# Divisions four chunks ahead, and weights and residuals loaded during the attentions, in two output projections

## The chip, the cores and the metric

One core of a Trainium2 chip runs the whole kernel in one launch. The metric is the time on the device in microseconds (us), lower is better. Five engines work side by side, each through its own queue in order: TensorE (PE: matmuls and transposes), VectorE (DVE), ScalarE (ACT), GpSimd (POOL) and SyncE (SP, which here only issues DMAs). They meet through semaphores.

## The reference

x is [2, 256, 48, 48], that is 2 images of 2304 positions and 256 channels. Two layers follow each other; all is float32.

```python
# layer 0: top-k attention, 8 heads of 32, and an MLP of 1x1 convolutions with batch norm
q, k, v = heads(Wq x + bq), heads(Wk x + bk), heads(Wv x + bv)
scores = q k^T * 32 ** -0.5
kth = top_k(scores, 64)[..., -1:]
attn = softmax(where(scores >= kth, scores, min))
o = Wo (attn v) + bo + x
h1 = relu(batchnorm(W1 o + b1));  h2 = batchnorm(W2 h1 + b2)       # 1024 hidden channels
x1 = h2 + o
# layer 1: RMS norm over channels, full attention, output projection
q, k, v = split(w_qkv (x1 / |x1| * g * 16))
out = w_out (softmax(q * 32 ** -0.5 k^T) v) + b_out + x1
```

## The kernel before

`build()` runs seven stages, each a block of its own with one program per engine; an engine leaves a block when all of it is done, so stages do not overlap except by what they load.

1. `project_heads` (layer 0) writes queries and keys, split in a high and a rest part, to DRAM (`q_parts`, `k_parts`) and keeps the values in `v_top`, which lies in the same memory as the big buffer `xs`.
2. `attention_top`: 8 heads times 18 pairs of 128-query tiles. SP loads keys and queries per head (`load_key_parts`, `load_query_parts`); GpSimd copies a head's values out of `v_all` into `v_s` and counts `v_ready`, twice per head. The unnormalised outputs are kept in `o_top`, and the sums of the exponentials in `sums`.
3. `project_out` (L707): 4608 positions in nine chunks of 512. It divides by the sums, turns the outputs so that channels lie on partitions, multiplies by Wo and adds bias and x.
4. `mlp`: first matrix (L874), statistics, relu (L924), second matrix (L889), statistics, x1 and the norm of layer 1. x1 is written to DRAM. One buffer `m_w` holds in turn the first matrix, the second (L859) and the three of the next layer (L818).
5. `project_heads` (layer 1) out of that buffer.
6. `attention_full`: as 2, with a full softmax; its values lie in `v_all`.
7. `output` (L1283): as 3, with w_out, b_out and, as residual, x1 read back from DRAM into `y` (2 transfers of 2304 KB); each finished piece of a chunk is stored to `out`.

The bodies of 3 and 7 are alike. VectorE computes one reciprocal of all 288 sums per partition (L779, L1366), divides chunks 0 and 1 (L777, L1364) and then, for each chunk, does the two adds (L791, L1377; they read the projection from PSUM and write over the residual) and divides chunk c + 2. TensorE turns chunk c + 1 (`turn`: eight transposes, L743, L1331) and projects chunk c (four matmuls of 128x128 by 512, which the trace shows as eight records, L758, L1345). ScalarE copies the turned chunk from PSUM into one of two buffers `a` (L770, L1357); it waits for projection c - 2 before it writes over a buffer. There are four PSUM banks for turned blocks and four for projections. SP issues all loads of such a stage when it begins: in 3 w_o, b_o, x in three pieces (into `xs`, where the values lay before) and the first MLP weights with seven vectors; in 7 w_out, b_out and y. VectorE waits for w and, in 7, for all of y (L1371) before its first add.

Of the kernel before, what the change touches and what calls it, by code (L numbers as in the profile page):

```python
# [26 lines left out]
P = 128  # L27
B, C, N = 2, 256, 48 * 48
KC = C // P
# [243 lines left out]
def attention_top(nc, cst, operands, q_parts, k_parts, v_all, o_all, sums):  # L273
# [5 lines left out]
    with ctx:  # L279
# [45 lines left out]
        def _(sync):  # L325
# [14 lines left out]
            per_head(HEADS - 1, HEADS - 1)  # L340
            for n in range(AHEAD_Q):
                sync.wait_ge(q_loaded[n], 32 * (HEADS * HEAD_PAIRS // AHEAD_Q + 1))
# [364 lines left out]
def project_out(nc, cst, xs, o_all, sums, x, w_o, b_o, mlp_weights, next_sources):  # L707
# [4 lines left out]
    with ctx:  # L712
        sb = lambda name, shape, dt=F32: ctx.enter_context(nc.sbuf_tensor("r_" + name, shape, dt))
        sem = lambda name: ctx.enter_context(nc.semaphore("r_" + name))
        w, bias = sb("w", [P, KC, C]), sb("bias", [P, KC])
# [4 lines left out]
        w_loaded, x_loaded = sem("w_loaded"), [sem(f"x_loaded{n}") for n in range(len(X_PIECES))]  # L720
# [52 lines left out]
        def _(dve):  # L773
# [5 lines left out]
            dve.reciprocal(one_by_sum[:, :, :], sums[:, :, :]).then_inc(inverse_ready, 1)  # L779
            dve.wait_ge(inverse_ready, 1)  # L780
            divide(0)
            divide(1)
            dve.wait_ge(w_loaded, 32)
            for c in range(NCH):
# [8 lines left out]
                if c + 2 < NCH:  # L793
                    divide(c + 2)
# [27 lines left out]
def mlp(nc, cst, xs, x1, weights, w_2, next_sources):  # L822
# [5 lines left out]
    with ctx:  # L828
# [5 lines left out]
        w2_s = w[:, :].rearrange("p (k c) -> p k c", k=MT)  # L834
# [185 lines left out]
def attention_full(nc, cst, operands, q_parts, k_parts, v_all, o_all, sums):  # L1020
# [7 lines left out]
    with ctx:  # L1028
# [22 lines left out]
        def _(sync):  # L1051
# [14 lines left out]
            per_head(HEADS - 1, HEADS - 1)  # L1066
            for n in range(AHEAD_Q):
                sync.wait_ge(q_loaded[n], 32 * (HEADS * HEAD_PAIRS // AHEAD_Q + 1))
# [214 lines left out]
def output(nc, cst, o_all, sums, x1, w_out, b_out, out):  # L1283
# [4 lines left out]
    with ctx:  # L1288
        sb = lambda name, shape, dt=F32: ctx.enter_context(nc.sbuf_tensor("o_" + name, shape, dt))
        sem = lambda name: ctx.enter_context(nc.semaphore("o_" + name))  # L1290
        w, bias = sb("w", [P, KC, C]), sb("bias", [P, KC])
        one_by_sum = sb("one_by_sum", [P, B * MCH, HEADS])
        a, y = [sb(f"a{n}", [P, KC, CW]) for n in range(2)], sb("y", [P, KC, B * N])
        ps_t = [ctx.enter_context(nc.psum_tensor(f"o_ps_t{n}", [P, CW], F32)) for n in range(4)]
        ps = [ctx.enter_context(nc.psum_tensor(f"o_ps{n}", [P, CW], F32)) for n in range(4)]
        w_loaded, x_loaded = sem("w_loaded"), sem("x_loaded")
# [152 lines left out]
```

## Time and profile before

| | us |
|---|---|
| median of 3 runs | 5311.72 (5310.89 to 5313.05) |
| profiled execution | 5306.61 |
| its span, first to last instruction | 5304.80 |

| engine | busy us | share of the span |
|---|---|---|
| TensorE | 4161.1 | 78% |
| VectorE | 4384.5 | 83% |
| ScalarE | 4144.0 | 78% |
| GpSimd | 1502.1 | 28% |

Where the stages lie in the span: the first attention ends at about 3378, project_out at 3441, mlp at 3772, the second attention at about 5231, output at 5304.8. The granted TensorE clock is a mean of 0.825 of its full 2.4 GHz over the span; a stretch at 0.5 is one at 1.2 GHz. Starts are us from the span's start. A row's "idle before" is the time for which its engine had nothing to do just before it, and behind the arrow stands what ended that.

### The profile page before, as it was taken

Reading aid. Unit: us, or ns where it says so; the run is one execution under the profiler, and the core shown is the slowest. Engines: PE = TensorE matmul, PEld = TensorE weight load, DVE = VectorE, ACT = ScalarE, POOL = GpSimd, SP = SyncE. Lnnn points to the kernel's source line nnn. Section 1 sums busy time; section 2 is a strip of 40 time slices with the busy share of each in tenths; the row PEclk is TensorE's granted clock in tenths of the full one; section 3 lists DMA queues with packets and bytes.
Section 4 is the critical chain, followed back from the end, with each engine's and each line's share of the span. In section 5 each row is a group of like instructions: output and inputs, shape, how many; then the busy total and the mean of one; then the engine's idle time right before and its main releaser. Section 6 shows DMA issues by size and latency. Waiting matters only on the chain. (4 is left out here: it accounts for less than half of the span.)

```text
span 5304.8 us, 112543 instructions
## 1 busy us (share of the span) xinstructions
PE 4161.1 (78%) x32161; PEld 2808.6 (53%) x32161; DVE 4384.5 (83%) x25258; ACT 4144.0 (78%) x6082; POOL 1502.1 (28%) x362
## 2 busy tenths in 40 slices
PE   8576477776777557767777667798999999999997
PEld 4344345444444334444454445443567777777774
DVE  4899999998999899999999999430378888888885
ACT  2798599988998678988999889544268888888884
POOL 0354354444454334444454445100100000000000
PEclk9677677777777777777777777899799999999999
DMA  5000000000000000000000000100320101111012
GB/s 208 6 17 16 5 16 8 18 16 7 18 17 16 7 15 8 17 16 8 17 17 9 17 16 8 56 8 6 143 77 25 34 24 33 33 25 34 24 33 89
DMA packets 79566, 154.52 MB, mean 29 GB/s; under 512 B 8120, under 2 KB 49464, under 8 KB 73528
## 3 DMA queue, kind: packets, MB, share of 16 engines
q1 hardware_dynamic: 78904, 146.72, 9.8%
q8 instruction: 290, 4.75, 0.4%
q14 instruction: 372, 3.05, 0.2%
HBM read 99.50 MB, written 47.19 MB: 28 GB/s over the span
## 5 line engine op out<-in xcount | busy, mean ns | idle before, releaser
L539 POOL TENSOR_TENSOR a_probs<-a_scores,a_probs 128x2304 f32<-128x2304 f32 x288 | 1460.1, 5092 | 1778.5 <-ACT a_probs L462 1778.5
L557 DVE MAX8 a_top<-a_scores 128x8 f32<-128x36 f32 x18432 | 1830.8, 179 | 46.8 <-ACT a_scores L446 46.1
L373 PE MATMUL a_ps_t<-ident,a_probs 128*128 128x128 f32 x5184 | 973.7, 325 | 704.0 <-ACT a_probs_t L457 570.1
L373 PEld LDWEIGHTS a_ps_t<-ident,a_probs 128*128 128x128 f32 x5184 | 672.6, 164 | 992.2 <-ACT a_probs_t L457 708.6
L462 ACT ACTIVATE a_probs<-a_scores,a_steep_kth 128x2304 f32<-128x2304 f32 x290 | 641.2, 2211 | 295.0 <-DVE a_minus_max L667 295.0
L1117 PE MATMUL b_ps_t<-ident,b_soft 128*128 128x128 f32 x5184 | 744.1, 279 | 20.9 <-issue 19.3
L1242 DVE TENSOR_SCALAR_CACHE_REDUCE b_soft<-b_ps_s 128x2304 f32<-128x2304 f32 x288 | 735.2, 2553 | 26.9 <-PE b_ps_s L1101 9.0
L457 ACT ACTIVATE a_probs_t<-a_ps_t 128x512 f32<-128x512 f32 (+1 forms) x1440 | 727.2, 545 | 20.4 <-PE a_ps_t L373 7.4
L1117 PEld LDWEIGHTS b_ps_t<-ident,b_soft 128*128 128x128 f32 x5184 | 581.0, 141 | 204.0 <-issue 80.4
L1199 ACT ACTIVATE b_soft<-b_soft,b_minus_max 128x2304 f32<-128x2304 f32 x288 | 638.1, 2216 | 43.6 <-issue 26.0
L450 ACT ACTIVATE a_probs<-a_probs,a_minus_max 128x2304 f32<-128x2304 f32 x288 | 638.0, 2215 | 28.6 <-issue 18.5
L363 PE MATMUL a_ps_s<-a_k_stack,a_q_ring 128*128 128x512 f32 (+1 forms) x1465 | 647.5, 601 | 14.7 <-ACT a_scores L446 9.8
L446 ACT ACTIVATE a_scores<-a_ps_s 128x2304 f32<-128x2304 f32 x292 | 607.0, 2079 | 12.3 <-PE a_ps_s L363 12.3
L382 PE MATMUL a_ps_o<-a_probs_t,a_v 128*32 128x128 f32 x10368 | 579.0, 303 | 0.2
L1206 ACT ACTIVATE b_soft_t<-b_ps_t 128x512 f32<-128x512 f32 (+1 forms) x864 | 419.4, 520 | 174.6 <-PE b_ps_t L1117 174.3
L363 PEld LDWEIGHTS a_ps_s<-a_k_stack,a_q_ring 128*128 128x128 f32 x1465 | 433.2, 319 | 156.6 <-ACT a_scores L446 64.5
L1101 PE MATMUL b_ps_s<-b_k_stack,b_q_ring 128*128 128x512 f32 (+1 forms) x1440 | 451.0, 411 | 8.4 <-DVE b_soft L1242 5.0
L1248 DVE COPY b_soft_t<-b_ps_t 128x512 f32<-128x512 f32 x576 | 385.1, 687 | 83.1 <-PE b_ps_t L1117 82.7
L382 PEld LDWEIGHTS a_ps_o<-a_probs_t,a_v 128*32 128x32 f32 x10368 | 263.0, 115 | 226.0 <-issue 113.7
L1078 POOL COPY b_v<-v_all 128x576 f32 x16 | 10.6, 667 | 1293.1 <-PE b_ps_o L1136 1185.8
L1136 PE MATMUL b_ps_o<-b_soft_t,b_v 128*32 128x256 f32 x5184 | 368.5, 384 | 0.6 <-issue 0.6
L401 PE MATMUL a_ps_o<-add_up,a_parts 128*128 128x32 f32 x576 | 148.6, 397 | 259.1 <-ACT a_parts L522 259.1
(128 smaller groups left out, 4216.7 us busy)
## 6 DMA issues: line engine op xcount, KB each, us to landing
a_k_stack<-k_parts SPq DMA_DIRECT2D x72, 288.0 KB, 6.0
b_k_stack<-k_parts SPq DMA_DIRECT2D x72, 288.0 KB, 6.1
a_q_ring<-q_parts SPq DMA_DIRECT2D x294, 64.0 KB
b_q_ring<-q_parts SPq DMA_DIRECT2D x294, 64.0 KB
k_parts<-p_high SPq DMA_DIRECT2D x36, 256.0 KB, 2.1
k_parts<-p_rest SPq DMA_DIRECT2D x36, 256.0 KB, 2.2
q_parts<-p_high SPq DMA_DIRECT2D x36, 256.0 KB, 2.0
q_parts<-p_rest SPq DMA_DIRECT2D x36, 256.0 KB, 2.0
```

The source lines that it names most:

```text
L363: last = pe.matmul(ps_s[:, c:c + n], q_ring[pair % AHEAD_Q][:, P * (s % 2):P * (s % 2) + P], k_stack[b][:, c:c + n], start=True, stop=True)
L373: last = pe.transpose(ps_t[(NTG * s + g) % 2][:, P * m:P * m + P], probs[s % 2][:, P * (m0 + m):P * (m0 + m) + P], cst["ident"][:, :])
L382: last = pe.matmul(ps_o[rows, P * (s % 2):P * (s % 2) + P], v_s[s // MCH][:, m, :], probs_t[:, m, :], start=m < 4, stop=m + 4 >= MCH)
L446: act.activation(scores_all[:, s % 4, :], ps_s[:, 0:N], ACT.Copy).then_inc(scores_kept, 1)
L450: act.activation(probs[s % 2][:, :], probs[s % 2][:, :], ACT.Exp, scale=SCALE, bias=minus_max[parity][:, s % 2:s % 2 + 1], accum_out=sums[ ...
L457: act.activation(probs_t[:, m0:m0 + n, :], ps_t[(NTG * s + g) % 2][:, 0:n * P].rearrange("p (m q) -> p m q", q=P), ACT.Copy).then_inc(turn ...
L462: act.activation(probs[u][:, :], scores_all[:, 2 * parity + u, :], ACT.Relu, scale=-STEEP, bias=steep_kth[parity][:, u:u + 1]).then_inc(pe ...
L539: pool.tensor_tensor(probs[u][:, :], scores_all[:, 2 * (p % 2) + u, :], probs[u][:, :], ALU.subtract).then_inc(masked_ready, 1)
L557: last = dve.max(top8[s // 2 % 2][:, s % 2, c, :], scores_all[:, s % 4, CHUNK * c:CHUNK * c + CHUNK])
L1117: last = pe.transpose(ps_t[(NTG * s + g) % 2][:, P * m:P * m + P], soft[s % 3][:, P * (m0 + m):P * (m0 + m) + P], cst["ident"][:, :])
L1199: act.activation(soft[s % 3][:, :], soft[s % 3][:, :], ACT.Exp, scale=-1.0, bias=minus_max[s % 3][:, 0:1], accum_out=sums[:, s, cols(h + a ...
L1242: dve.tensor_scalar(soft[s % 3][:, :], ps_s[:, 0:N], -SCALE, None, ALU.mult, ALU.min, accum_out=minus_max[s % 3][:, 0:1]).then_inc(shifted ...
```

## The change

- Both projections: the reciprocal is split in the part of chunk 0 (32 sums per partition) and the rest (256). Division 0 follows the first part, divisions 1 to 3 the second, and in the loop chunk c + 4 is divided behind chunk c.
- A class `ProjectionOut` holds weights, bias and their semaphores outside of the stage. The loads that SP issued when the stage began are issued in a function `load_ahead` by SP at the end of its program in the attention before, after a wait for `v_ready` to be full (all values have been copied out): for project_out also x into `xs` and the first MLP weights, for output also y.
- y now lies in `v_all` of the second attention, which is kept beyond it, and w_out in the buffer of the key weights of layer 1. w and bias of project_out are allocated ahead of the attention's tiles.
- mlp: the second matrix has a buffer of its own (8 KB per partition), and its load is issued at the start of the stage. The loads of the next layer's weights wait for the first matrix to be done instead of the second.

```diff
@@ attention_top and attention_full, SP
             per_head(HEADS - 1, HEADS - 1)
+            sync.wait_ge(v_ready, HEADS * B)
+            load_ahead(sync)
@@
+DIVIDED_AHEAD = 4
+class ProjectionOut:
+    def __init__(self, nc, ctx, layer, w=None):
+        sb = lambda name, shape: ctx.enter_context(nc.sbuf_tensor(layer + name, shape, F32))
+        self.w = sb("w", [P, KC, C]) if w is None else w
+        self.bias = sb("bias", [P, KC])
+        self.w_loaded = ctx.enter_context(nc.semaphore(layer + "w_loaded"))
+        self.x_loaded = [ctx.enter_context(nc.semaphore(f"{layer}x_loaded{n}")) for n in range(len(X_PIECES))]
+    def load(self, sync, w, bias):
+        sync.dma_start(self.w[:, :, :], w.rearrange("(k p) o -> p k o", p=P)).then_inc(self.w_loaded, 16)
+        sync.dma_start(self.bias[:, :], bias).then_inc(self.w_loaded, 16)
@@ project_out
-        @block.sync
-        def _(sync):
-            sync.dma_start(w[:, :, :], w_o.rearrange("(k p) o -> p k o", p=P)).then_inc(w_loaded, 16)
-            sync.dma_start(bias[:, :], b_o).then_inc(w_loaded, 16)
-            for n in range(len(X_PIECES)):
-                load_x(sync, xs, x, n, x_loaded)
-            mlp_weights.load(sync, next_sources)
@@ project_out and output, VectorE
-            dve.reciprocal(one_by_sum[:, :, :], sums[:, :, :]).then_inc(inverse_ready, 1)
+            dve.reciprocal(one_by_sum[:, 0:4, :], sums[:, 0:4, :]).then_inc(inverse_ready, 1)
             dve.wait_ge(inverse_ready, 1)
             divide(0)
-            divide(1)
+            dve.reciprocal(one_by_sum[:, 4:B * MCH, :], sums[:, 4:B * MCH, :]).then_inc(inverse_ready, 1)
+            dve.wait_ge(inverse_ready, 2)
+            for c in range(1, DIVIDED_AHEAD):
+                divide(c)
@@
-                if c + 2 < NCH:
-                    divide(c + 2)
+                if c + DIVIDED_AHEAD < NCH:
+                    divide(c + DIVIDED_AHEAD)
@@ mlp
-        w2_s = w[:, :].rearrange("p (k c) -> p k c", k=MT)
+        w2_s = sb("w2", [P, MT, C])
@@
+            sync.dma_start(w2_s[:, :, :], w_2.rearrange("(k p) o -> p k o", p=P)).then_inc(w2_loaded, 16)
             sync.wait_ge(hid_done, NCH * MT)
-            sync.dma_start(w2_s, w_2.rearrange("(k p) o -> p k o", p=P)).then_inc(w2_loaded, 16)
-            sync.wait_ge(y_done, NCH * KC)
             weights.load_next(sync, next_sources)
@@ output, SP
-            sync.dma_start(w[:, :, :], w_out.rearrange("(k p) o -> p k o", p=P)).then_inc(w_loaded, 16)
-            sync.dma_start(bias[:, :], b_out).then_inc(w_loaded, 16)
-            for kc in range(KC):
-                sync.dma_start(y[:, kc, :], x1[kc * P:kc * P + P, :]).then_inc(x_loaded, 16)
@@ build
+            projection = ProjectionOut(nc, top, "r_")
+            def load_ahead(sync):
+                projection.load(sync, t["w_o"], t["b_o"])
+                for n in range(len(X_PIECES)):
+                    load_x(sync, xs, t["x"], n, projection.x_loaded)
+                mlp_weights.load(sync, t)
@@
+        v_all = ctx.enter_context(nc.sbuf_tensor("v_all", [P, B * MCH, C], F32))
+        y = v_all[:, :, :].rearrange("p m c -> p (m c)").rearrange("p (k n) -> p k n", k=KC)
+        projection = ProjectionOut(nc, ctx, "o_", mlp_weights.next_w[:, 0, :, :])
@@
+            def load_ahead(sync):
+                projection.load(sync, t["w_out"], t["b_out"])
+                for kc in range(KC):
+                    sync.dma_start(y[:, kc, :], x1[kc * P:kc * P + P, :]).then_inc(projection.x_loaded[0], 16)
```

## Rows read from the trace of the kernel before

**Rows 1.** The page's first line: the span and its instructions.

```profile
span 5304.8 us, 112543 instructions
```

**Rows 2.** The chain of waits that ended last: start us, us, what; its one transfer.

```profile
5233.25 15.22 DMA o_y<-x
```

**Rows 3.** Timeline of output(): start us, us, engine, line, out<-in, count [idle before, releaser].

```profile
5231.60 1.95 DVE L1366 RECIPROCAL o_one_by_sum<-xs 128x288 f32<-128x288 f32 x1 [0.33 <-PEq L1028]
...
5234.96 3.24 PE L1331 MATMUL o_ps_t<-ident,o_all 128*128 128x128 f32 x16 [4.15 <-DVE o_all L1364]
...
5238.04 3.60 PE L1345 MATMUL o_ps<-o_a,o_w 128*128 128x512 f32 x8
...
5258.12 1.22 DVE L1364 TENSOR_TENSOR o_all<-o_all,o_one_by_sum 128x1024 f32<-128x1024 f32 x1
...
5259.39 1.09 PE L1331 MATMUL o_ps_t<-ident,o_all 128*128 128x128 f32 x8 [1.98 <-DVE o_all L1364]
...
5260.32 3.60 PE L1345 MATMUL o_ps<-o_a,o_w 128*128 128x512 f32 x8
...
5263.96 0.75 DVE L1377 SCALAR_TENSOR_TENSOR o_y<-o_ps,o_bias,o_y 128x512 f32<-128x512 f32 x1 [0.97 <-PE o_ps L1345]
...
5264.62 1.22 DVE L1364 TENSOR_TENSOR o_all<-o_all,o_one_by_sum 128x1024 f32<-128x1024 f32 x1
...
5301.60 0.75 DVE L1377 SCALAR_TENSOR_TENSOR o_y<-o_ps,o_bias,o_y 128x512 f32<-128x512 f32 x1 [0.96 <-PE o_ps L1345]
```

**Rows 4.** One line's instructions (L1010): durations in ns, minimum/median/maximum, first and last start.

```profile
L1010 DVE RECIPROCAL m_norm<-m_norm x1: 378/378/378, 3747.6 to 3747.6; 128x36 f32<-128x36 f32 x1
```

**Rows 5.** Timeline of project_out(), same columns; its head, second projection and last add.

```profile
3378.15 1.95 DVE L779 RECIPROCAL r_one_by_sum<-sums_top 128x288 f32<-128x288 f32 x1 [29.63 <-PEq L279]
...
3380.13 2.36 DVE L777 TENSOR_TENSOR o_top<-o_top,r_one_by_sum 128x1024 f32<-128x1024 f32 x2
...
3381.41 3.31 PE L743 MATMUL r_ps_t<-ident,o_top 128*128 128x128 f32 x16 [3.59 <-DVE o_top L777]
...
3384.56 3.60 PE L758 MATMUL r_ps<-r_a,r_w 128*128 128x512 f32 x8
...
3391.08 5.28 PE L758 MATMUL r_ps<-r_a,r_w 128*128 128x512 f32 x8
...
3440.54 0.75 DVE L791 SCALAR_TENSOR_TENSOR xs<-r_ps,r_bias,xs 128x512 f32<-128x512 f32 x1 [0.97 <-PE r_ps L758]
```

**Rows 6.** Stretches: length, busy us (instructions) by engine, granted clock, DMA share, GB/s.

```profile
3378.00:3385.00 7.00, 3.59 (x18) 3.35 (x19) 4.31 (x3) 1.92 (x4) 0.00 (x0) 0.56 0.80 257
3385.00:3392.00 7.00, 5.02 (x18) 2.48 (x17) 2.63 (x3) 1.45 (x3) 0.00 (x0) 0.93 1.02 427
3480.00:3520.00 40.00, 40.00 (x95) 17.75 (x94) 16.12 (x24) 16.04 (x24) 0.00 (x0) 1.00 0.00 0
```

**Rows 7.** Timeline of SP's queue: the last key loads of both attentions.

```profile
3322.83 1.90 SPq L145 DMA_DIRECT2D a_k_stack<-k_parts  x4
5216.58 1.83 SPq L145 DMA_DIRECT2D b_k_stack<-k_parts  x4
```

**Rows 8.** Timeline of GpSimd: two pairs of tiles of the first attention's last head.

```profile
3309.88 10.14 POOL L539 TENSOR_TENSOR a_probs<-a_scores,a_probs 128x2304 f32<-128x2304 f32 x2 [10.76 <-ACT a_probs L462]
3330.36 10.14 POOL L539 TENSOR_TENSOR a_probs<-a_scores,a_probs 128x2304 f32<-128x2304 f32 x2 [10.34 <-ACT a_probs L462]
```

**Rows 9.** Second MLP weights: their load by its line and its landing; what started then.

```profile
L859 SPq DMA_DIRECT2D m_w<-w x1: 378/378/378, 3566.0 to 3566.0; - x1
DMA to landing us min/median/max: 5.4/5.4/5.4
3571.09 11.38 ACT L924 ACTIVATE m_hid<-m_hid,m_shift,m_scale 128x512 f32<-128x512 f32 x16 [0.87 <-DVE m_shift L986]
3572.05 13.48 PE L889 MATMUL m_ps_o<-m_hid,m_w 128*128 x27 [6.05 <-ACT m_hid L924]
```

**Rows 10.** One line's instructions (L557), columns as in rows 4.

```profile
L557 DVE MAX8 a_top<-a_scores x18432: 168/179/201, 116.1 to 3338.3; 128x8 f32<-128x36 f32 x199
```

More of the change, by code:

```diff
@@ L704, in _, with project_out @@
             dve.sem_inc(kth_ready, 1)
-def project_out(nc, cst, xs, o_all, sums, x, w_o, b_o, mlp_weights, next_sources):
+DIVIDED_AHEAD = 4
[9 more added lines that the diff above has]
+        sync.dma_start(self.bias[:, :], bias).then_inc(self.w_loaded, 16)
+def project_out(nc, cst, xs, o_all, sums, projection):
     CW = BANK
@@ L714, in project_out @@
         sem = lambda name: ctx.enter_context(nc.semaphore("r_" + name))
-        w, bias = sb("w", [P, KC, C]), sb("bias", [P, KC])
+        w, bias, w_loaded, x_loaded = projection.w, projection.bias, projection.w_loaded, projection.x_loaded
         one_by_sum = sb("one_by_sum", [P, B * MCH, HEADS])
@@ L1066, in _ @@
             per_head(HEADS - 1, HEADS - 1)
+            sync.wait_ge(v_ready, HEADS * B)
+            load_ahead(sync)
             for n in range(AHEAD_Q):
@@ L1280, in _, with output @@
                 add_quadrants(p, HEADS - 1, (HEADS - 1) * HEAD_PAIRS + p)
-def output(nc, cst, o_all, sums, x1, w_out, b_out, out):
+def output(nc, cst, o_all, sums, y, projection, out):
     CW = BANK
@@ L1290, in output @@
         sem = lambda name: ctx.enter_context(nc.semaphore("o_" + name))
-        w, bias = sb("w", [P, KC, C]), sb("bias", [P, KC])
+        w, bias, w_loaded, x_loaded = projection.w, projection.bias, projection.w_loaded, projection.x_loaded[0]
         one_by_sum = sb("one_by_sum", [P, B * MCH, HEADS])
-        a, y = [sb(f"a{n}", [P, KC, CW]) for n in range(2)], sb("y", [P, KC, B * N])
+        a = [sb(f"a{n}", [P, KC, CW]) for n in range(2)]
         ps_t = [ctx.enter_context(nc.psum_tensor(f"o_ps_t{n}", [P, CW], F32)) for n in range(4)]
         ps = [ctx.enter_context(nc.psum_tensor(f"o_ps{n}", [P, CW], F32)) for n in range(4)]
-        w_loaded, x_loaded = sem("w_loaded"), sem("x_loaded")
         turned, a_ready, proj_done, added, stored = (sem("turned"), sem("a_ready"), sem("proj_done"), sem("added"),
@@ L1364, in divide @@
                 dve.tensor_tensor(o_c, o_c, inverse_c, ALU.mult).then_inc(divided, 1)
-            dve.reciprocal(one_by_sum[:, :, :], sums[:, :, :]).then_inc(inverse_ready, 1)
+            dve.reciprocal(one_by_sum[:, 0:4, :], sums[:, 0:4, :]).then_inc(inverse_ready, 1)
             dve.wait_ge(inverse_ready, 1)
             divide(0)
-            divide(1)
+            dve.reciprocal(one_by_sum[:, 4:B * MCH, :], sums[:, 4:B * MCH, :]).then_inc(inverse_ready, 1)
+            dve.wait_ge(inverse_ready, 2)
+            for c in range(1, DIVIDED_AHEAD):
+                divide(c)
             dve.wait_ge(w_loaded, 32)
@@ L1402, in build @@
             sums = top.enter_context(nc.sbuf_tensor("sums_top", [P, B * MCH, HEADS], F32))
-            attention_top(nc, cst, operands, q_parts, k_parts, v_top, o_top, sums)
-            project_out(nc, cst, xs, o_top, sums, t["x"], t["w_o"], t["b_o"], mlp_weights, t)
+            projection = ProjectionOut(nc, top, "r_")
[4 more added lines that the diff above has]
+                mlp_weights.load(sync, t)
+            attention_top(nc, cst, operands, q_parts, k_parts, v_top, o_top, sums, load_ahead)
+            project_out(nc, cst, xs, o_top, sums, projection)
         mlp(nc, cst, xs, x1, mlp_weights, t["w_2"], (t["w_k1"], t["w_q1"], t["w_v1"]))
@@ L1407, in build @@
         sums = xs[:, 0, 0, 0:B * MCH * HEADS].rearrange("p (m h) -> p m h", h=HEADS)
+        v_all = ctx.enter_context(nc.sbuf_tensor("v_all", [P, B * MCH, C], F32))
+        y = v_all[:, :, :].rearrange("p m c -> p (m c)").rearrange("p (k n) -> p k n", k=KC)
+        projection = ProjectionOut(nc, ctx, "o_", mlp_weights.next_w[:, 0, :, :])
         with ExitStack() as full:
             operands = Operands(nc, full, "b_")
-            v_all = full.enter_context(nc.sbuf_tensor("v_all", [P, B * MCH, C], F32))
             project_heads(nc, xs, mlp_weights.next_w, mlp_weights.next_loaded, operands, q_parts, k_parts, v_all)
-            attention_full(nc, cst, operands, q_parts, k_parts, v_all, o_all, sums)
-        output(nc, cst, o_all, sums, x1, t["w_out"], t["b_out"], out)
+            def load_ahead(sync):
+                projection.load(sync, t["w_out"], t["b_out"])
+                for kc in range(KC):
+                    sync.dma_start(y[:, kc, :], x1[kc * P:kc * P + P, :]).then_inc(projection.x_loaded[0], 16)
+            attention_full(nc, cst, operands, q_parts, k_parts, v_all, o_all, sums, load_ahead)
+        output(nc, cst, o_all, sums, y, projection, out)
 def per_partition(v, rows=P):
```

9 lines of the change are left out of this document (4 added, 5 removed).

## The prediction

> **What bounds the kernel now.** I looked first at the span [rows 1]; the profiled execution took 5306.61 us around a span of 5304.80 us, and the median of the runs shown is 5311.72 us, so the sum below is made on the profiled execution and its difference is carried to the median. The page's share of busy time says little here: the two attentions fill some 4,600 us of the span (the first ends at 3378, the second takes the 1,350 us up to 5231), and this change does not edit what they do. It edits the two short stages behind them and one load inside the MLP. So the second view is the chain that ended last. It shows one transfer of 15.22 us, the residual y of the last stage, on which everything waits [rows 2]. The third view is the timeline of the two stages.
>
> In a steady chunk of output() [rows 3] there are four links in a circle: VectorE divides a chunk (starts 5258.12), TensorE turns it (5259.39), TensorE projects it (5260.32), VectorE adds bias and residual (last one 5263.96), and only then divides the next: 5264.62, which is 6.50 us after the first. TensorE itself is needed for the stretch from 5259.39 to 5263.75: 0.93 us for eight transposes, then eight matmul records that start 0.43 us apart (the row's 3.60 us is seven such steps and the last one's modelled 0.59 us), 3.43 us; the last add starts 0.21 us after that. That is 4.36 us. The other 2.14 us of each period TensorE waits for a division that could have been made earlier. project_out() has the same body. This is the idle time to win.
>
> **Part 1: divisions four chunks ahead.** What is late next, if the division is not? Per chunk VectorE has two adds of 0.75 us and one division of 1.22 us, 2.7 us; ScalarE two copies of 0.6 us; both fit under 4.36 us. The two a buffers let ScalarE fill chunk c+1 once projection c-1 is done, which is just when its transposes are done, and it has the 3.43 us of projection c for 1.2 us of copies. So TensorE is next, back to back: nine projections of 3.43 us, and the seven turns of chunks 2 to 8 between them at 0.93 us: 30.87 + 6.51 = 37.38 us from the first projection on.
>
> The head of each stage gets a reciprocal in two parts. A reciprocal of 36 elements took 0.38 us [rows 4], one of 288 took 1.95 us [rows 5]; between them an element costs 0.0062 us, so 32 elements are 0.36 us and 256 are 1.75 us (estimates from those rows). In project_out: VectorE starts at 3378.15, division 0 at 3378.54 instead of 3380.13, ending 3379.75. Then comes the second reciprocal (3379.69 to 3381.44), and division 1 ends at 3382.69, where it ended at 3382.5 before: the first turn is earlier, the second is not. TensorE turned 16 blocks in 3.15 us at the start [rows 5], thus 8 in 1.58 us, and the first projection starts at 3382.75 + 1.58 = 3384.33 (before: 3384.56). The same working in output [rows 3], from 5231.60: second turn at 5236.19, plus 1.54 us, first projection at 5237.73 (before: 5238.04). Divisions 2 and 3 now stand ahead of the first add on VectorE's queue; they end 2.4 us after division 1, at 3385.1 and 5238.6, and the first add is released 1.7 us into the first projection, at the earliest at 3386.0 and 5239.4, so nobody waits for them.
>
> **The clock at the head.** From 3378 to 3385 the granted clock was 0.56 and thereafter mostly near 1.0, and under a steadily busy TensorE (3480 to 3520) it was 1.00 [rows 6]. In project_out the second projection ran low: eight matmuls in 5.28 us, 5.11 us by the same count, where 3.43 is the full-speed figure [rows 5], 1.7 us more. Before, the 16 transposes came in one piece ahead of the first projection; now there is a hole of 1.3 us between the two turns, so the first projection may also run low. Its price is 0 to 1.7 us; no row is nearer to one end, and I take the middle, 0.85 us, once per stage. Later dips I put at none, because the waits that precede them go.
> The Trainium skill (TensorE: Matmul & The Clock Gate, HAM oscillation) says that a kernel which alternates short bursts with waits is throttled again and again. The trace agrees (0.56 in the first window, 1.00 in the dense MLP), and by that rule alone the sum would be the same without the 0.85 us in each head.
>
> project_out: 3384.33 + 0.85 + 37.38 + 0.21 = 3422.77 for the start of the last add, against 3440.54 [rows 5]: 17.8 us. MLP follows that add as before.
> output: 5237.73 + 0.85 + 37.38 + 0.21 = 5276.17 against 5301.60 [rows 3]: 25.4 us. What follows the last add (its 0.75 us, the last store, the end) stays.
>
> **Part 2: weights and residuals loaded while the attentions still run.** In project_out this brings nothing by itself: the first projection waited for the second turn, and no add waited for x (all adds there are released by TensorE). In output it is needed, or the 25.4 us are not to be had: the first add stood until y had landed at 5248.47 [rows 2]. The loads are queued on SP behind the last key loads, which are issued by 3324.73 and 5218.41 [rows 7]. The wait on v_ready ahead of them is for copies made at the start of the last head, so it holds nothing. In the first attention some 5.8 MB follow; y moved 4.7 MB in 15.2 us, so these take about 19 us and end some 30 us before that stage starts. In the second, y is issued at about 5219.4 and lands between 5234.6 and, with the 1.2 MB of keys still ahead of it at the same rate, 5238.5. The first add wants it at 5239.4; TensorE would first be stopped at the projection of chunk 2, which needs the first of four PSUM banks back, at about 5247.3. So there is some 9 us of cover, and y costs nothing until it is used up.
> Their cost for the attentions: the first attention does one pair of tiles per 20.5 to 20.9 us, its head set by the chain ScalarE to GpSimd. The pair before the last key loads took 10.76 + 10.14 us, that which contains them 10.34 + 10.14 us [rows 8]: 1.2 MB beside it cost nothing that shows. For 5.8 MB I take zero, with 0 to 2 us as range (five times nothing, and less than one tile's 5 us of GpSimd). The tail of the second attention is 13 us; same figure.
> The SP queue holds nothing else there; in output its first store waits for the first add as before.
>
> **Part 3: second MLP weights in their own buffer.** Their load was issued at 3566.0 and landed 5.4 us later, about 3571.8 with the issue; ScalarE began the relu of the first block at 3571.09, which takes 0.79 us, and TensorE started at 3572.05 [rows 9]. Both arrived together, so with the load gone the relu ends the wait: 0 to 0.2 us, I take 0. The next layer's weights are issued after the first half instead of the second; they were in place long before their use, 0 us. The w_2 load at the MLP's start lies beside 120 us of matmuls.
>
> **Sum.** 17.8 + 25.4 + 0 = 43.2 us. Profiled execution: 5306.6 - 43.2 = 5263.4 us. Median: 5311.7 - 43.2 = 5268.5 us.
>
> **Rivals.**
> 1. *The switch into output() comes late*, because y is still in flight when it happens (before, no stage ended with a large load outstanding). If the end of a stage waits for it, the new stage starts when y lands, up to 5238.5 instead of 5231.5: +7 us, 5275.5. Against it: nothing in the program asks for that wait, and with y in flight from 5233 on the first turns and the projection ran with no idle time but for divisions. Chance 0.07.
> The Trainium skill (DMA: Bandwidth & Descriptors, Queues, rings and completion order) lets every DMA engine take turns among the queues with work, so instruction fetches would have to share with y; that would act at the same place, with the same bound. No row here shows it.
> 2. *The clock dips go on* in the denser stages: two of 1.7 us in each, as the old ones had: +6.8 us, 5275.3. For it: dips also fell in output at 70% busy. Against: the dense MLP. Chance 0.08.
> 3. *The division was not the link*: the period stays at 6.5 us, say because TensorE is held by the ScalarE copies. Then only y's wait goes, 5248.5 to about 5239.8: 8.7 us, 5303.0. The copies' slack speaks against it. Chance 0.04.
> 4. *Slower*: the new tiles are allocated ahead of both attentions and move all of theirs to other SBUF addresses. If one bulk instruction is sensitive to that, it pays 18,432 times: MAX8 of 179 ns [rows 10] is the bound of the first attention, so 2.4 ns more each eats the whole 43 us, and 3 ns, 1.7%, gives +55 - 43 = 12 us slower, 5324. Against it: its median covers four score buffers at different addresses. Chance 0.04.
> Forecast 0.76; 0.01 for more than forecast.
>
> **How the numbers follow.** The likeliest is 5268.5. Bounds of the unknown costs: heads -1.7 to +1.7, attentions beside loads 0 to +4, and the attentions' own change from run to run and with the moved code, some 0.1% of 4,600 us or 5 us either way. With rivals 1 and 2 inside, the range is 5258 to 5282. A measurement of this kernel can tell 0.2%, 10.6 us, from no change. Faster: forecast, rivals 1 and 2, more: 0.92. Same: rival 3 and a quarter of rival 4, 0.05. Slower: the rest of rival 4, 0.03.
>
> **What would show it.** In the changed kernel, projection to projection in both stages every 4.36 us, TensorE busy throughout and no wait for divisions; y landed by 5239 with the adds released by TensorE; first projection about 6 us into each stage; TensorE's wait ahead of the second MLP half unchanged; pairs of 20.5 us in the last head during the loads; MAX8 at 179 ns. The prediction is wrong if a stage starts more than 1 us after the attention's last instruction, if the period stays above 5 us, or if the attentions' lengths change by more than 5 us.

## The result, and the profile after

| | before, us | changed, us |
|---|---|---|
| median, first comparison | 5311.31 (4 runs) | 5261.05 (4 runs) |
| median, second comparison | 5304.92 (15 runs) | 5264.03 (5 runs) |
| profiled execution | 5306.61 | 5257.19 |
| its span | 5304.8 | 5255.4 |

The ratio is 0.9904 (0.9891 to 0.9916) in the first comparison and 0.9923 (0.9910 to 0.9937) in the second. The change takes 50 us off in the one and 41 us in the other; 43.2 had been forecast. Where they went, from the two first profiles; a projection stage is counted from its first VectorE instruction to the start of its last add:

| stretch | before | changed | difference |
|---|---|---|---|
| up to project_out | 3378.2 | 3376.2 | -2.0 |
| project_out | 62.4 | 45.2 | -17.2 |
| from there to the second attention's first matmul | 435.9 | 433.9 | -2.0 |
| second attention | 1355.2 | 1352.2 | -2.9 |
| output | 70.0 | 44.3 | -25.7 |
| end | 3.2 | 3.6 | +0.5 |

The two edited stages give 42.9 us. The other 6.5 us lie where the prediction had put nothing. The lengths come from unrounded times, so a difference can stand 0.1 us off its row.

The timeline of project_out in the changed kernel (start us, us, engine, line, out<-in, count [idle before, releaser]):

```profile
3376.15 0.35 DVE L790 RECIPROCAL r_one_by_sum<-sums_top 128x32 f32<-128x32 f32 x1 [29.61 <-PEq L279]
...
3376.54 1.22 DVE L788 TENSOR_TENSOR o_top<-o_top,r_one_by_sum 128x1024 f32<-128x1024 f32 x1
...
3377.82 1.97 PE L754 MATMUL r_ps_t<-ident,o_top 128*128 128x128 f32 x8 [1.99 <-DVE o_top L788]
...
3379.46 3.50 DVE L788 TENSOR_TENSOR o_top<-o_top,r_one_by_sum 128x1024 f32<-128x1024 f32 x3
...
3380.84 1.94 PE L754 MATMUL r_ps_t<-ident,o_top 128*128 128x128 f32 x8 [1.05 <-DVE o_top L788]
...
3382.57 5.14 PE L769 MATMUL r_ps<-r_a,r_w 128*128 128x512 f32 x8
...
3387.55 1.04 PE L754 MATMUL r_ps_t<-ident,o_top 128*128 128x128 f32 x8
...
3388.42 3.60 PE L769 MATMUL r_ps<-r_a,r_w 128*128 128x512 f32 x8
...
3391.85 1.04 PE L754 MATMUL r_ps_t<-ident,o_top 128*128 128x128 f32 x8
...
3392.73 3.60 PE L769 MATMUL r_ps<-r_a,r_w 128*128 128x512 f32 x8
...
3421.34 0.75 DVE L805 SCALAR_TENSOR_TENSOR xs<-r_ps,r_bias,xs 128x512 f32<-128x512 f32 x1 [0.97 <-PE r_ps L769]
```

This is rows 5 after the change. The turn of a chunk (3387.55) and its projection (3388.42) follow each other without an idle time, and the next pair comes 4.31 us later (3392.73): no bracket names a division any more. The first projection took 5.14 us where the later ones take 3.60, and both turns took nearly 2 us where the later ones take 1.04: that is the head at low clock.

The same for output, where rows 3 and 2 answer:

```profile
5206.71 0.42 DVE L1271 TENSOR_REDUCE o_all<-b_ps_o 128x64 f32<-128x256 f32 x1 [3.41 <-PE b_ps_o L1161]
...
5207.46 0.35 DVE L1376 RECIPROCAL o_one_by_sum<-xs 128x32 f32<-128x32 f32 x1 [0.32 <-PEq L1041]
...
5213.82 4.29 PE L1355 MATMUL o_ps<-o_a,m_w 128*128 128x512 f32 x8
...
5217.15 0.75 DVE L1390 SCALAR_TENSOR_TENSOR v_all<-o_ps,o_bias,v_all 128x512 f32<-128x512 f32 x1 [2.88 <-DMA v_all<-x]
...
5217.95 1.04 PE L1341 MATMUL o_ps_t<-ident,o_all 128*128 128x128 f32 x8
...
5218.82 3.60 PE L1355 MATMUL o_ps<-o_a,m_w 128*128 128x512 f32 x8
...
5251.75 0.75 DVE L1390 SCALAR_TENSOR_TENSOR v_all<-o_ps,o_bias,v_all 128x512 f32<-128x512 f32 x1 [0.97 <-PE o_ps L1355]
```

y now ends a wait of 2.88 us of VectorE (5217.15), which TensorE does not notice: its next turn (5217.95) comes straight after the first projection. The last row stands 44.3 us after the stage's first reciprocal (5207.46), and that reciprocal 0.75 us after the attention's last reduction began (5206.71). The same gap was there before (5230.85 to 5231.60).

Stretches of the changed kernel (length; busy us and instructions of PE, PEld, DVE, ACT, POOL; granted clock, DMA share, GB/s), which answer to rows 6:

```profile
5194.00:5198.00 4.00, 3.36 (x39) 2.01 (x38) 1.62 (x3) 3.22 (x4) 0.00 (x0) 1.00 1.05 215
5202.00:5206.00 4.00, 3.08 (x40) 1.67 (x39) 0.42 (x1) 0.91 (x3) 0.00 (x0) 1.00 1.01 356
5206.00:5210.00 4.00, 1.22 (x6) 1.01 (x7) 2.93 (x4) 0.18 (x1) 0.00 (x0) 0.80 1.00 421
3376.00:3383.00 7.00, 4.13 (x17) 3.67 (x18) 6.74 (x6) 1.98 (x4) 0.00 (x0) 0.50 0.01 4
3376.00:3385.50 9.50, 6.63 (x20) 4.68 (x21) 6.74 (x6) 2.39 (x4) 0.00 (x0) 0.50 0.01 3
3390.00:3420.00 30.00, 30.00 (x107) 15.94 (x106) 15.41 (x19) 6.51 (x12) 0.00 (x0) 1.00 0.00 0
```

The granted clock is 0.50, the lower of the two levels, throughout project_out's head, up to 3385.5, and 1.00, the full 2.4 GHz, from 3390 on, with TensorE busy for 30.00 of 30.00 us.

### The profile page after: what moved, and what is told of

It reads as the page before. It is cut to its first block and busy times, and to the rows that moved or that the text cites. A ratio compares the mean times of both kernels' runs of the same rounds, so it can differ in the third digit from the quotient of the medians.

```text
span 5255.4 us, 112545 instructions
## 1 busy us (share of the span) xinstructions
PE 4144.9 (79%) x32161; PEld 2800.8 (53%) x32161; DVE 4385.3 (83%) x25260; ACT 4141.6 (79%) x6082; POOL 1501.7 (29%) x362
## 5 line engine op out<-in xcount | busy, mean ns | idle before, releaser
L365 PEld LDWEIGHTS a_ps_s<-a_k_stack,a_q_ring 128*128 128x128 f32 x1465 | 433.9, 320 | 157.2 <-ACT a_scores L448 64.3
L1263 DVE COPY b_soft_t<-b_ps_t 128x512 f32<-128x512 f32 x576 | 384.9, 686 | 81.9 <-PE b_ps_t L1132 81.2
```

Source lines behind the costliest of these rows:

```text
L365: last = pe.matmul(ps_s[:, c:c + n], q_ring[pair % AHEAD_Q][:, P * (s % 2):P * (s % 2) + P], k_stack[b][:, c:c + n], start=True, stop=True)
```

## Experiments

**Divisions alone, loads alone, and both kernels again.** The first takes only these lines into the kernel before (in both stages):

```diff
-            dve.reciprocal(one_by_sum[:, :, :], sums[:, :, :]).then_inc(inverse_ready, 1)
+            dve.reciprocal(one_by_sum[:, 0:4, :], sums[:, 0:4, :]).then_inc(inverse_ready, 1)
...
-                if c + 2 < NCH:
-                    divide(c + 2)
+                if c + DIVIDED_AHEAD < NCH:
+                    divide(c + DIVIDED_AHEAD)
```

> The kernel before with only the divisions four chunks ahead (and the reciprocal in two parts); all loads where they were, second MLP weights in the shared buffer. Theory A (the loads are nearly worthless once the divisions are ahead, because y is only late when the PSUM banks run out): project_out from its first VectorE instruction to its last add 45.2 us as in the changed kernel (62.4 before), output 46.3 us against 44.3 in the changed kernel (70.0 before), since y lands 16.9 us into the stage and the projection of chunk 2 would want its bank at 15.7: in all -41 us, about 5270. Theory B (as the prediction put it, without the early y the gain of output is not to be had): the first add waits for y and everything behind it moves with it, output 44.3 + 7.2 = 51.5 us or more, in all -36 us or less. Theory C (the some 7 us by which the attentions were shorter in the changed kernel come from the early loads and moved tiles, not from chance): the attentions are as long here as before.

Measured: 5265.83 against 5304.92 us, ratio 0.9930 (0.9916 to 0.9943), 39 us less. project_out 45.1, output 45.7 us. Theory A holds and B falls. Its timeline shows the mechanism:

```profile
5236.15 1.04 PE L1337 MATMUL o_ps_t<-ident,o_all 128*128 128x128 f32 x8
...
5237.31 1.41 DVE L1386 SCALAR_TENSOR_TENSOR o_y<-o_ps,o_bias,o_y 128x512 f32<-128x512 f32 x2 [9.30 <-DMA o_y<-x]
...
5238.20 3.67 PE L1351 MATMUL o_ps<-o_a,o_w 128*128 128x512 f32 x8 [1.02 <-DVE o_y L1386]
```

y is late here nearly as much as before: the first add starts 16.1 us into the stage (17.0 before). But by then TensorE has projected two chunks and turned a third, and it stands still for 1.02 us only, until the first add frees a PSUM bank. Against the changed kernel, timed beside it (5264.03 us), all the early loads are worth 1.8 us by the medians, which is less than either kernel's own spread.

The second is the changed kernel with the old divisions (`DIVIDED_AHEAD = 2`, one reciprocal) and the second MLP weights back in the shared buffer.

> The changed kernel with the divisions two chunks ahead and one reciprocal as before, and the second MLP weights in the shared buffer: the early loads alone. Theory A: project_out 62.4 us as before (its first projection waits for the second turn, not for a load); output: first add at 9.7 us instead of 17.0 into the stage, 70.0 - 7.2 = 62.8 us; in all -7 us, about 5304. Theory C (early loads and moved tiles shorten the attentions by some 7 us): -14 us, about 5297, and the stretches outside of the two projections are 7 us shorter than before.

Measured: 5294.59 us, ratio 0.9982 (0.9973 to 0.9991), 10 us less. project_out 62.4, output 61.7 us (first add at 10.1 us). So project_out gets nothing from its loads, and output 8.3 us if they come alone, but only 1.4 us on top of the divisions (45.7 to 44.3). The two parts are not additive: they fill the same wait.

> The changed kernel unaltered, timed beside the others. The two projection stages at 45.2 and 44.3 us again, to 0.3 us. If the 7 us outside of them are chance, their sum differs from the first profile by some us and the median's difference to before is nearer 43 us than 50 (theory A); if they belong to the change, it is 50 again (theory C).

> The kernel before unaltered, profiled once more. The two stages 62.4 and 70.0 us again, to 0.3 us. By theory A the first attention (up to project_out's first VectorE instruction, 3378.2 us in the first profile), the stretch from MLP to the second attention and the second attention (1355.2 us) differ from the first profile by 2 to 4 us; by theory C they are the same to 0.5 us.

Measured: changed kernel 5264.03 us, stages 45.2 and 44.4; kernel before, one execution, stages 62.4 and 69.8 us. Outside of them the changed kernel was 5175.1 us in this profile and 5165.9 in the first, the kernel before 5173.6 and 5172.4. Two executions of one kernel thus differ by up to 9 us where nothing was edited. That is theory A's chance. The kernel before, though, differed in its three stretches by 1.0, 0.9 and 1.0 us only, which neither theory had said, and the second attention was the shorter one in every profile with the early loads, which left a share for theory C.

**Where the unforecast microseconds are.** The tiles of both attentions lie elsewhere in the changed kernel. This run moves them in the kernel before, and nothing else:

```diff
+            top.enter_context(nc.sbuf_tensor("moved_w", [P, KC, C], F32))
+            top.enter_context(nc.sbuf_tensor("moved_bias", [P, KC], F32))
             attention_top(nc, cst, operands, q_parts, k_parts, v_top, o_top, sums)
...
+        v_all = ctx.enter_context(nc.sbuf_tensor("v_all", [P, B * MCH, C], F32))
+        ctx.enter_context(nc.sbuf_tensor("moved_bias2", [P, KC], F32))
         with ExitStack() as full:
             operands = Operands(nc, full, "b_")
-            v_all = full.enter_context(nc.sbuf_tensor("v_all", [P, B * MCH, C], F32))
```

> The kernel before with nothing changed but the places of its tiles: room for w_o's copy and two biases is taken ahead of the attentions' tiles and v_all is allocated ahead of the second attention's, as in the changed kernel. In three profiles without the early loads the second attention lasted 1355.2 to 1357.6 us, in seven with them 1348.0 to 1354.8 us. Theory D (the moved tiles make it some 5 us shorter): 1350 to 1354 us here, and some 5 us off the time of before. Theory E (what makes it shorter is something else, the early loads or where the instructions lie, or it is chance): 1355 to 1358 us here, the time of before within its spread. MAX8 stays at 179 ns by both.

Measured: 5305.96 against 5312.59 us, ratio 0.9990 (0.9980 to 1.0000); second attention 1351.6 us; MAX8 179 ns. The interval just touches no change, but w2_only (below), timed beside it with its tiles at the old places, took 5312.03 us, 6 us more as well. Over all profiles in which the head loop is kept:

| second attention's tiles | us in each profile |
|---|---|
| as before | 1355.2, 1356.2, 1357.6, 1360.2 |
| moved | 1352.2, 1354.8, 1351.5, 1351.0, 1348.0, 1350.3, 1350.9, 1351.6 |

The two groups do not overlap, and the last of the moved ones has no early loads. So the edit that moves the tiles makes the second attention some 5 us shorter, theory D; by which instruction, and by what mechanism, is not shown. What can be seen is where. GpSimd copies a head's values twice per head (start, us, ..., [idle before]); in the kernel before:

```profile
4146.96 0.67 POOL L1078 COPY b_v<-v_all 128x576 f32 x1 [86.25 <-PE b_ps_o L1136]
4228.97 0.67 POOL L1078 COPY b_v<-v_all 128x576 f32 x1 [81.35 <-PE b_ps_o L1136]
```

From copy to copy it is 82.0 us where the head loop does not turn (4146.96 to 4228.97) and 86.9 us where it does (the first row's 86.25 us of idle time and the 0.67 us of the copy before it). The 82.0 us repeat to 0.1 us in the changed kernel and in most others; the six halves with a turn lie between 85.1 and 88.4 us. Added up they are 519.8 to 523.1 us in the four profiles with the old places and 514.2 to 519.6 us in the eight with moved ones, 5 us less in the mean: the second attention's gain sits in them. ScalarE's exponentials (L1199) show the turn as idle time without a releaser, six times in sum; kernel before, then the one with moved tiles:

```profile
  issue: 26.0, 6
```

```profile
  issue: 24.7, 6
```

It was 25.8 to 26.0 us in all four profiles with the old places and 24.7 to 24.9 us in the four with moved ones that were looked at: a trace of the effect, a fifth of its size. The instructions' own places in memory may have moved with the tiles; that was not separated.

**The second MLP weights alone.**

> The kernel before with only the second MLP weights in their own buffer. Prediction's step: TensorE's wait ahead of the second half of the MLP is ended by the relu of its first block, so from the last ScalarE copy of the first half to the first matmul of the second it takes 5.9 us as before (3566.13 to 3572.05), and the time is that of before. Rival (the load ended the wait by a little): up to 0.2 us less, which no timing can tell but the profile can. The second attention: 1355 to 1358 us by theory D, since no tile of it moves.

Measured: 5312.03 against 5312.59 us, ratio 0.9999 (0.9989 to 1.0009). From the last ScalarE copy (3567.57) to the first matmul (3573.50) it is 5.93 us there, 5.92 us before. The same rows in the changed kernel, to be laid beside rows 9:

```profile
3546.76 0.69 ACT L929 ACTIVATE m_hid<-m_ps_h,m_b 128x512 f32 x1 [1.03 <-PE m_ps_h L887]
...
3551.73 5.04 ACT L937 ACTIVATE m_hid<-m_hid,m_shift,m_scale 128x512 f32<-128x512 f32 x7 [0.88 <-DVE m_shift L999]
...
3552.69 3.77 PE L902 MATMUL m_ps_o<-m_hid,m_w 128*128 x4 [6.06 <-ACT m_hid L937]
```

The relu releases TensorE, whether the weights came early or at the last moment. This part of the change is worth nothing, as forecast. The second attention lasted 1360.2 us, the longest of all and more than the 1355 to 1358 expected; its half heads without a turn were 82.25 us.

**How much cover y has.** 3.5 MB more are queued ahead of y:

```diff
                 projection.load(sync, t["w_out"], t["b_out"])
+                sync.dma_start(xs[:, 1, :, :].rearrange("p b n -> p (b n)"), x1[0:P, :]).then_inc(unused, 16)
+                sync.dma_start(xs[:, 0, 1, :], x1[P:2 * P, 0:N]).then_inc(unused, 16)
```

> The changed kernel with 3.5 MB more loaded ahead of y (x1 into a part of xs that nobody reads then; extra work, nothing left out): y lands some 8 to 9 us later, about 18 to 19 us into output instead of 9.6. Theory A (TensorE is stopped only at the projection of chunk 2, 15.7 us into the stage, by a PSUM bank that the first add frees 0.9 us after y has landed): output 44.3 + (18.5 + 0.9 - 15.7) = 48 us, so most of the delay is hidden. Theory B (each us of y is a us of the stage): 53 us.

Measured, in one execution: first add 17.7 us into the stage, output 48.9 us, where theory A had 48 and theory B 53:

```profile
5222.63 1.04 PE L1341 MATMUL o_ps_t<-ident,o_all 128*128 128x128 f32 x8
...
5224.72 1.41 DVE L1390 SCALAR_TENSOR_TENSOR v_all<-o_ps,o_bias,v_all 128x512 f32<-128x512 f32 x2 [10.85 <-DMA v_all<-x]
...
5225.61 5.37 PE L1355 MATMUL o_ps<-o_a,m_w 128*128 128x512 f32 x8 [1.94 <-DVE v_all L1390]
```

y is 8.0 us later, and TensorE stands for 1.94 us. The rest is the clock: behind the stop the projection took 5.37 us instead of 3.60, and the first one of the stage 5.08 against 4.29. 1.9 + 1.8 + 0.8 make 4.5 of the 4.7 us. The 0.8 us are not y's, for that projection comes before the stop, and the next run has them with y where it was. So 8.0 us of delay cost 3.7 us, and 44.3 + 3.7 is theory A's 48.

**Three chunks ahead.** One constant, `DIVIDED_AHEAD = 3`.

> The changed kernel with the divisions three chunks ahead instead of four. Theory A: the division of chunk c+1 is already made while projection c-1 runs, so one chunk more than before breaks the circle: 4.31 us per chunk, stages of 45.2 and 44.3 us as with four. Rival (it takes the fourth to cover the adds that queue on VectorE while y is late): output longer by one division, 1.2 us, or more.

Measured, in one execution: 45.2 and 45.1 us. The period is 4.31 us as with four; output's 0.8 us are those of its first projection, 5.10 against 4.29 us, and no cost of the third chunk: with four ahead it took 5.08 us in y_behind_more. In output that projection thus differs from execution to execution. But see the next kernel.

**Better heads.** First the reciprocal is cut behind chunk 1:

```diff
-            dve.reciprocal(one_by_sum[:, 0:4, :], sums[:, 0:4, :]).then_inc(inverse_ready, 1)
+            dve.reciprocal(one_by_sum[:, 0:8, :], sums[:, 0:8, :]).then_inc(inverse_ready, 1)
             dve.wait_ge(inverse_ready, 1)
             divide(0)
+            divide(1)
```

> The changed kernel with the reciprocal cut behind chunk 1 instead of chunk 0: division 1 no longer waits for the long second part. Theory A (the head of each stage is VectorE's chain into the second turn, and the low clock of the first projection comes from the hole between the two turns): the reciprocal of 64 elements takes 0.55 us, both turns run in one piece, the first projection starts 5.0 us into the stage instead of 6.4 and runs at full speed (3.4 us instead of 5.0 and 4.1): stages of 42.2 and 42.2 us instead of 45.2 and 44.3, in all -5 us, about 5259 where the changed kernel has 5264. Rival (the clock in the head is set by what came before the stage): the first projection still runs low in part, 43.8 and 43 us, -2.8 us.

Measured: 5259.71 against 5310.22 us, ratio 0.9905 (0.9888 to 0.9921); stages 42.9 and 43.9 us, 2.6 us less than the changed kernel's in sum. The sum, 86.8 us, is the rival's, but the two stages tell different things. The first projection starts at 5.3 and 5.4 us and took 3.96 and 4.88 us, where the changed kernel's took 5.14 and 4.29. In project_out the clock came up earlier (stretches as above, project_out from 3378.59, then output from 5206.22):

```profile
3378.60:3384.50 5.90, 4.04 (x17) 3.81 (x18) 5.83 (x6) 2.12 (x4) 0.00 (x0) 0.50 0.01 4
3385.00:3388.00 3.00, 3.00 (x10) 1.37 (x9) 1.23 (x3) 0.00 (x0) 0.00 (x0) 1.00 0.00 0
5207.50:5214.00 6.50, 5.82 (x19) 4.48 (x20) 5.50 (x5) 2.39 (x4) 0.00 (x0) 0.50 0.56 236
```

It was at 1.00 from 6.4 us into the stage, where the changed kernel was at 0.50 for 9.4 us. The kernel before says the same: its turns come in one piece too, and its first projection, 6.4 us into the stage like the changed kernel's, took 3.60 us against 5.14 (rows 5). So in project_out the hole between the turns did keep the clock low. In output it did not: without the hole the clock was still 0.50 up to 7.8 us into the stage, and the projection, which starts 1.0 us earlier, spent more of its time there. The kernel before had no hole there either, and its first projection took 3.60 us in one profile and 4.87 us in the other.

Then, with three chunks ahead, extra work for TensorE while it waits for division 0:

```diff
+            for n in range(10):
+                pe.transpose(ps_t[3][:, 0:P], cst["ident"][:, :], cst["ident"][:, :])
             turn(0)
```

> As split_at_two, with divisions three chunks ahead, and with ten transposes of the identity into a bank nobody reads at the start of both stages, while TensorE waits for division 0 (extra work, nothing left out). If TensorE's activity ahead of the first turn is what brings the clock up, the turns run at full speed too (8 in 0.9 us instead of 1.6) and the first projection starts 4.0 us into the stage: 41.2 us each, another -1 us a stage. If ten transposes are not enough for that, the stages are as in split_at_two to 0.3 us.

Measured: 5254.85 us, ratio 0.9895 (0.9879 to 0.9912); stages 41.5 and 42.0 us. Its timeline in project_out, and the stretch of output:

```profile
3380.34 2.37 PE L759 MATMUL r_ps_t<-ident 128*128 128x128 f32 x10 [0.32 <-PEq L279]
...
3382.50 2.15 PE L754 MATMUL r_ps_t<-ident,o_top 128*128 128x128 f32 x16
...
3384.52 3.70 PE L771 MATMUL r_ps<-r_a,r_w 128*128 128x512 f32 x8
```

```profile
5204.00:5246.00 42.00, 40.72 (x154) 22.05 (x154) 24.89 (x28) 9.77 (x18) 0.00 (x0) 1.00 0.41 157
```

Ten transposes that nobody reads take 2.37 us, and the sixteen real ones behind them 2.15 us, where they took 3.31 us before (rows 5) and 3.68 us in split_at_two; the first projection is at 3.70 us. In output the clock did not fall at all, 1.00 for the whole stage. That stage is now short enough for y to be felt:

```profile
5213.90 1.41 DVE L1396 SCALAR_TENSOR_TENSOR v_all<-o_ps,o_bias,v_all 128x512 f32<-128x512 f32 x2 [4.20 <-DMA v_all<-x]
...
5216.49 1.09 PE L1344 MATMUL o_ps_t<-ident,o_all 128*128 128x128 f32 x8 [0.63 <-DVE o_all L1379]
```

The turn of chunk 3 waits for its division, which stands on VectorE behind the adds that waited for y. In the next kernel, also with three ahead, y let the first add go at 9.1 us instead of 9.9 us into the stage; this turn did not wait, and the stage took 41.3 us, 0.8 us less. By the order of VectorE's queue a fourth chunk would have been divided ahead of those adds, so it should have a use when the residual is late; warm heads with four ahead were not run.

**The head loops written out.** The turn of the loop had been named as the place of the chance. On top of split_warm:

```diff
-            with pe.Fori(0, HEADS - 1) as h:
+            for h in range(HEADS - 1):
```

and so on every engine of attention_full; in the second kernel also in attention_top.

> split_warm with the loop over the heads of the second attention written out on all its engines (the same work in the same order, no loop). In all profiles so far half a head lasts 82.0 us where no loop turns and 85.2 to 88.2 us where one does, and those are the stretches by which executions differ. Theory A (the turn of the loop is both that cost and the chance that stood beside the 43 us): every half head at 82.0 us, the second attention shorter by 7 x 4.4 = 31 us, about 1318 us instead of 1348 to 1358, in all about 5224, and its length repeats to 1 us. Rival (it is not the turn itself but fetching instructions that costs, and straight code has more to fetch): stalls in other places, gain under 15 us or a loss.

> As heads_written_out, and the loops over the heads of the first attention written out too (its branches on doubtful thresholds stay). There the turn shows as one pair of tiles in 18 of 22.8 to 23.5 us instead of 20.5 to 20.9. Theory A: 7 x 2.6 = 18 us less again, the first attention to about 3361 us, in all about 5206. Rival (VectorE's straight code of some 170 short instructions per pair outruns its fetching): the pairs get longer than 20.9 us and the first attention loses more than 18 us.

Measured: 5228.33 us, ratio 0.9848 (0.9835 to 0.9862), and 5195.99 us, ratio 0.9786 (0.9772 to 0.9799), both against 5309.22. In the first the second attention took 1321.4 us, and its copies come every 81.75 us:

```profile
4200.89 0.67 POOL L1096 COPY b_v<-v_all 128x576 f32<-128x576 f32 x1 [81.08 <-PE b_ps_o L1154]
4282.64 0.67 POOL L1096 COPY b_v<-v_all 128x576 f32<-128x576 f32 x1 [81.08 <-PE b_ps_o L1154]
```

The second attention is 27 us shorter than in split_warm (1348.0), where 31 had been forecast from seven turns. The loops of TensorE, ScalarE and VectorE jump back only six times, and six at 4.4 us are 26. Of the 27 us, 24 lie in the six halves with a turn; the halves without one went from 82.01 to 81.75 us. So in the second attention the turn is nearly all of the gain.

In the first attention it is 29 us (3380.1 to 3350.8) where 18 had been forecast. There GpSimd's pair at a turn, 22.6 to 23.7 us long in the kernel with that loop, takes 20.4 to 20.9 us: seven turns give 19 us, as forecast. The other 10 us are spread over the rest, where the usual pair of 20.5 us is mostly 20.4; their cause is open. The last kernel's second attention took 1325.9 us, 4.4 us more than the first one's, so its length did not repeat to 1 us.

The usual pairs took 20.4 to 21.2 us written out and 20.5 to 21.4 us with the loop, and every half head 81.75 us in the first kernel and 81.9 us in the second, so the rival, stalls of the straight code, does not show. The runs of the last kernel lie between 5193.6 and 5198.7 us. Whether it also repeats better is not shown: its five runs spread by 5 us, but the changed kernel's spread by 6 us in the first comparison (four runs) and 14 in the second (five). It is 1.2 or 1.4% faster than the changed kernel, by which of that kernel's two ratios is taken.

## Why the prediction was right, and where not

**The circle through the division: right.** Period 4.31 us where 4.36 was forecast and 6.50 measured before; TensorE is busy throughout, so rival 3 fell. project_out gained 17.2 us for 17.8, output 25.7 for 25.4. The part of the divisions alone is 39 us by its median. That the first median (5261.05) lies in the range is luck in part: the bounds listed for the unknown costs add up to 5261.8 at the lower end, and the range was put at 5258 without a reason for the rest.

**The heads: right in time, low in price.** The first projection starts 6.4 us into both stages, where 6.2 and 6.1 had been worked out. The first projection's low clock cost 1.5 and 0.7 us for the 0.85 taken. The step that picked a cause, the hole between the turns, was right for project_out and wrong for output: closing it (split_at_two) brought the full clock 3 us earlier in the one and not in the other, and keeping TensorE at work before the turns (split_warm) raised it in both. The Trainium skill (TensorE: Matmul & The Clock Gate, HAM oscillation) says that an engine which waits between short bursts starts the next one throttled; the trace agrees, 0.50 in project_out's head behind the waits and 1.00 from 3390 on, and the 5.37 us behind a stop of 1.94 us show it once more. No dips came later, so rival 2 fell.

**"The 25.4 us are not to be had" without the early y: wrong.** This is the step of the prediction that failed. The prediction had the number that contradicts it: TensorE is stopped at the projection of chunk 2, about 15.7 us into the stage, and y landed 16.9 us into it even when loaded late. The difference is a loss of one to two microseconds, and 1.4 was measured. I had read the first add's 12.6 us of waiting as time of the stage:

```profile
5248.56 1.41 DVE L1377 SCALAR_TENSOR_TENSOR o_y<-o_ps,o_bias,o_y 128x512 f32<-128x512 f32 x2 [12.60 <-DMA o_y<-x]
```

It was, but only because each division stood behind the adds. The forecast of output came out all the same, because both parts were in the kernel together.

**y's landing: missed, without a price.** Issued by the rows below, it was to land at most 6.9 us into output and landed at 9.7:

```profile
5192.44 1.82 SPq L145 DMA_DIRECT2D b_k_stack<-k_parts  x4
...
5195.28 0.90 SPq L1441 DMA_DIRECT2D v_all<-x  x2
```

The keys and the end of the queue ahead of it do not run at y's rate. In the windows shown above the DMA engines are fully busy from 5194 on but move 215 GB/s at first, 356 and then 421 GB/s. The mistake was to charge the keys by their bytes: in the trace a packet of the keys (9,216 bytes) took 752 ns (the median) in the first of these windows, one of y (18,432 bytes) 689 ns in the last. The 9 us of cover, which had been counted from the landing, were nearer 6.

**The loads beside the attention: nothing, as taken.** GpSimd's last pairs in the changed kernel, with the loads in flight beside the second of them (6.0 MB in the units in which y is 4.7; the prediction had 5.8):

```profile
3307.91 10.14 POOL L541 TENSOR_TENSOR a_probs<-a_scores,a_probs 128x2304 f32<-128x2304 f32 x2 [10.79 <-ACT a_probs L464]
3328.39 10.15 POOL L541 TENSOR_TENSOR a_probs<-a_scores,a_probs 128x2304 f32<-128x2304 f32 x2 [10.35 <-ACT a_probs L464]
```

Idle and busy are those of rows 8 to 0.03 us. MAX8's median is 179 ns as in rows 10.

**The switch into output: not late.** Rival 1 fell: 0.75 us from the last reduction to the first reciprocal, with the DMA engines at a share of 1.00. The Trainium skill (DMA: Bandwidth & Descriptors, Queues, rings and completion order) has each DMA engine go round the queues with work, so instruction fetches would take turns with y's packets; the trace does not show a cost of it at this place.

**Rival 4 had the place right and the sign wrong.** Moving the tiles does change an attention, the second and not through MAX8, and by 5 us to the better. The range had 5 us either way for this and for chance together. The 43 us from the stages and some 5 from the moved tiles would make 48; the two comparisons gave 50 and 41, and two profiles of the changed kernel differ by 9 us outside of the stages. That the forecast of 43.2 lies between the two is no proof of its last microseconds.

## What to carry over

A stage whose steps hand one chunk round in a circle is sped up by taking one link out of the circle, and here one chunk more of lead did it; more lead can pay only where something else is late. Before a load is moved forward, look for the instruction that the late data stops on the engine that bounds the stage: with spare PSUM banks a residual that came 16 us into the stage, 6 us later than in the changed kernel, cost 1.4. The price of a loop's turn is worth reading off a profile by comparing stretches with and without it.

## What the runs showed of the hardware

- A turn of the head loop cost 3.1 to 6.2 us in the second attention, six times, with TensorE, ScalarE and VectorE idle together (kernel before: TensorE 19.3 us and ScalarE 26.0 us in sum). Written out, every half head between two copies took 81.75 us in one kernel and 81.9 us in the other. The turns are not where most of the chance lies: of the 9 us between the two profiles of the changed kernel, 6.0 lie in the first attention, where the seven pairs at a turn account for 1.1, and 2.6 in the second.
- Moving tiles in SBUF changed an attention of 1,355 us by some 5 us, with the same instructions and the same data; whether it is the tiles' places or the instructions' own is open.
- Ten transposes that nobody reads, put where TensorE waits anyway, brought the next sixteen from 3.7 to 2.15 us.
- The DMA engines' time can be full (share 1.05) at half the rate: 215 GB/s while the keys were loaded, 32 rows of 9,216 bytes at a time, against 421 GB/s with y's 128 rows of 18,432 bytes. Which of the two differences counts was not separated.
